# Slot attention in one block: context rows as values, fp32r updates, a second exponential

## The reference

```python
x_in = _ln(x, lnkv_g, lnkv_b)                  # x is the context here, 6404 rows
k = x_in @ wk + bk
v = x_in @ wv + bv
slots = q_mu + jnp.exp(q_logsig) * noise       # noise is the normed token
for _ in range(3):
    prev = slots
    q = _ln(slots, lnq_g, lnq_b) @ wq + bq
    logits = jnp.einsum('bnd,bkd->bnk', k, q) / scale
    attn = jax.nn.softmax(logits, axis=-1) + 1e-8      # over the slots
    attn = attn / jnp.sum(attn, axis=1, keepdims=True) # over the context
    upd = jnp.einsum('bnk,bnd->bkd', attn, v)
    slots = upd @ wu + bu + prev
    h = _ln(slots, lnm_g, lnm_b) @ w1 + b1
    slots = jax.nn.gelu(h, approximate=False) @ w2 + b2 + slots
    slots = _ln(slots + x_cls[:, None, :], lnp_g, lnp_b)
x = x + slots
```

## Time and profile before

| | |
|---|---|
| median of 3 runs | 3694.49 us (3694.09 to 3701.91) |
| profiled execution | 3696.8 us, its span 3695.0 us |
| TensorE busy | 3261.3 us (88%) |
| VectorE busy | 2541.0 us (69%) |
| ScalarE busy | 1522.6 us (41%) |
| GpSimd busy | 1656.7 us (45%) |

### The profile page before, as it was taken

How to read it: one execution, slowest core, us unless ns; L and a number is a source line. 1 busy time by engine, 2 the same in 40 slices (tenths; PEclk the granted TensorE clock), 3 DMA queues, 4 the chain that set the end, 5 groups by cost and what they waited for, 6 DMA issues and landing times. The chain is left out here.

```text
span 3695.0 us, 52448 instructions
## 1 busy us (share of the span) xinstructions
PE 3261.3 (88%) x18307; PEld 1830.0 (50%) x18307; DVE 2541.0 (69%) x4276; ACT 1522.6 (41%) x1875; POOL 1656.7 (45%) x1085
## 2 busy tenths in 40 slices
PE   3795969848734899999999999999999999999977
PEld 2463635523332455555555555555555555555435
DVE  6786868765324877687687777777777768768531
ACT  4231323324411344444444544444444444444432
POOL 1222212211122265565565566566556556556750
PEclk9896979956667999999999999999999999999988
DMA  1000000000031000000000000000000000000000
GB/s 59 0 0 1 0 0 0 0 12 1 1 106 49 3 1 1 1 4 1 1 4 1 1 4 1 1 1 4 1 1 4 1 1 2 1 1 1 1 25 6
DMA packets 20393, 27.92 MB, mean 8 GB/s; under 512 B 5064, under 2 KB 12368, under 8 KB 20048
## 3 DMA queue, kind: packets, MB, share of 16 engines
q1 hardware_dynamic: 18832, 21.83, 1.8%
q0 software_dynamic: 1344, 3.15, 0.3%
HBM read 21.30 MB, written 3.67 MB: 7 GB/s over the span
## 5 line engine op out<-in xcount | busy, mean ns | idle before, releaser
L2017 ACT ACTIVATE pair_probs<-banks 128x1024 f32<-128x1024 f32 (+1 forms) x944 | 965.5, 1026 | 1035.9 <-PE banks L1927 984.0
L2066 DVE TENSOR_REDUCE pair_peaks<-banks 128x1 f32<-128x512 f32 (+1 forms) x1800 | 1086.0, 666 | 271.7 <-PE banks L1909 258.2
L2159 POOL TENSOR_TENSOR pair_total_pool<-pair_total_pool,pair_probs 128x1536 f32<-128x1536 f32 x208 | 724.6, 3484 | 754.0 <-DVE pair_total L2080 748.8
L1950 PE MATMUL banks<-pair_probs,pair_values 128*64 128x512 f32 (+1 forms) x3776 | 873.1, 600 | 0.0
L1909 PE MATMUL banks<-pair_k_high,pair_q_high 64*128 64x512 f32 (+1 forms) x1920 | 567.0, 441 | 27.4 <-DVE pair_peaks L2059 14.9
L2148 POOL TENSOR_TENSOR pair_total_pool<-pair_total_pool,pair_probs 128x1024 f32<-128x1024 f32 x224 | 536.0, 2393 | 39.1 <-POOL pair_total_pool L2159 20.6
L2080 DVE TENSOR_TENSOR pair_total<-pair_total,pair_probs 128x512 f32<-128x512 f32 (+2 forms) x464 | 457.9, 987 | 94.6 <-ACT pair_probs L2017 69.4
L1950 PEld LDWEIGHTS banks<-pair_probs,pair_values 128*64 128x64 f32 (+1 forms) x3776 | 248.3, 136 | 473.0 <-issue 385.1
L1927 PE MATMUL banks<-pair_q_shift,pair_one_rows 64*128 64x512 f32 (+1 forms) x1888 | 475.7, 396 | 3.1 <-ACT pair_probs L2017 3.1
L1909 PEld LDWEIGHTS banks<-pair_k_high,pair_q_high 64*128 64x128 f32 x1920 | 262.6, 184 | 356.3 <-issue 211.7
L1927 PE MATMUL banks<-pair_q_high,pair_k_high 64*128 64x512 f32 (+1 forms) x1888 | 427.0, 391 | 0.0
(11 more groups left out here) (312 smaller groups left out, 3484.8 us busy)
## 6 DMA issues: line engine op xcount, KB each, us to landing
expert_w<-in_fc SPq DMA_DIRECT2D x32, 256.0 KB, 3.7
context_rows<-in_ctx SPq DMA_DIRECT2D x10, 320.0 KB, 5.7
dense_w<-in_We SPq DMA_DIRECT2D x2, 1024.0 KB
experts_in<-expert_zeros SPq DMA_DIRECT2D x1, 1024.0 KB, 3.9
expert_b<-in_fc_b SPq DMA_DIRECT2D x2, 512.0 KB, 4.9
expert_rows<-experts_in SPq DMA_DIRECT2D x16, 64.0 KB, 2.0
experts_out<-expert_result POOLq DMA_DIRECT2D x4, 256.0 KB, 4.3
row_parameters<-in_rows SPq DMA_DIRECT2D x1, 896.0 KB, 7.8
```

The lines of the kernel that those rows point to most:

```text
L1950: last = pe.matmul(out[heads[head], :], values[0:n, ring_of(h // 2, i // 4), i % 4, heads[head]], probs_of(h, i)[0:n, head, :], start=i == ...
L2017: act.activation(probs_of(h, i)[0:n], slot(e)[0:n], ACT.Exp, scale=1.0 / 8.0).then_inc(S["expd"].sem, 1)
L2066: v.reduce_max(peaks[:, head, t, b:b + 1], fill_bank(f, head)[:, 0:width(b)], axis=AX).then_inc(S["peaked"].sem, 1)
L2159: pool.tensor_tensor(pooled[:], pooled[:], three, ALU.add).then_inc(S["pooled"].sem, 1)
```

## The change

The whole slot stage becomes one block with a pipeline written out by hand; the three loops are unrolled.

Preparation: each piece of the context is normed by ScalarE alone, transposed from its rows and kept in `k.zT`. Gain and shift of the context's norm are folded into the key weights (`wk`, `bias`), so the keys come straight from `k.zT`. Values are not made. The update sums context rows instead, and a matrix `combined` (value weights times wu, with the gain folded in) is applied after. The last column of each normed row is set to 1: since a normed row sums to zero the matrix can do without that column, and it now carries the sum of the attention, so `total` and L655 go. The statistics of x, the first slots and the first queries are made between the pieces.

Loop: keys are read from `k_high` and `k_low` without the ring. ScalarE takes the exponential twice from the same bank, once in fp32 with its sum (L546) and once written as fp32r (L549). The difference of the two is the low part: VectorE makes 768 columns of it (L654), GpSimd 256 (L781). GpSimd weighs the row tile (L769), rounds it (L772) and takes its low part (L774), in the first iteration it also adds up the rows (L817), and at tile 4 it adds `bu` to the slots (L820). TensorE's update is three fp32r products for each half (L451 to L453), three tiles behind the scores.

Between loops: the work is cut into two halves of four token tiles, which ScalarE, TensorE, GpSimd and VectorE take in turn, with no block's end. The reciprocal comes from the projected column 128 (L725). In `causal_` and `pair_` code, semaphores of the ended stage are used again, and waits count from their totals.

```diff
@@ slot_scores_and_updates (before) @@
-                    for n, source in enumerate((k_high, k_low)):
-                        pool.tensor_copy(key[:, r, n, 0:parts], source[:, ds(i * P, parts)]).then_inc(staged_s.sem, 1)
...
-                    for c in range(2):
-                        last = pe.matmul(update[:, c, :], value[0:parts, r, :], probs[0:parts, r, c * 512:(c + 1) * 512],
-                                         start=first, stop=final)
...
-                    v.scalar_tensor_tensor(out=total[0:parts], in0=probs[0:parts, r, :], scalar=small[0:parts, r, 3:4],
-                                           in1=total[0:parts], op0=ALU.mult, op1=ALU.add).then_inc(total_s.sem, 1)
@@ slot_attention (after), TensorE @@
+                def add(it, i):
+                    g, n, r = it * N + i, rows_of_tile(i), i % RING
+                    wait(pe, "valued", g + 1)
+                    wait(pe, "copied", g + 1)
+                    wait(pe, "subbed", g + 1)
+                    wait(pe, "subbed_pool", g + 1)
+                    for c in range(2):
+                        bank = k.ps[:, 4 + c, :]
+                        pe.matmul(bank, value_high[0:n, r, :], probs_high[0:n, r, columns[c]], start=i == 0, stop=False)
+                        pe.matmul(bank, value_low[0:n, r, :], probs_high[0:n, r, columns[c]], start=False, stop=False)
+                        last = pe.matmul(bank, value_high[0:n, r, :], probs_low[0:n, r, columns[c]], start=False, stop=i == CT)
+                    done("added", last)
@@ ScalarE @@
+                def exponential(it, i):
+                    g, n, r = it * N + i, rows_of_tile(i), i % RING
+                    wait(act, "bias", g + 1)
+                    wait(act, "subbed", g - RING + 1)
+                    wait(act, "subbed_pool", g - RING + 1)
+                    done("expd", act.activation(probs[0:n, r, :], flat(scores[r][0:n]), ACT.Exp, bias=small[0:n, r, 1:2],
+                                                scale=SLOT_SCALE, accum_out=small[0:n, r, 2:3]))
+                    wait(act, "added", g - RING + 1)
+                    done("copied", act.activation(probs_high[0:n, r, :], flat(scores[r][0:n]), ACT.Exp, bias=small[0:n, r, 1:2],
+                                                  scale=SLOT_SCALE))
@@ VectorE @@
+                def subtract(it, i):
+                    g, n, r = it * N + i, rows_of_tile(i), i % RING
+                    wait(v, "copied", g + 1)
+                    wait(v, "added", g - RING + 1)
+                    done("subbed", v.tensor_tensor(probs_low[0:n, r, 0:SHARE], probs[0:n, r, 0:SHARE],
+                                                   probs_high[0:n, r, 0:SHARE].bitcast(F32), ALU.subtract))
@@ GpSimd @@
+                def weigh(it, i):
+                    g, n, r = it * N + i, rows_of_tile(i), i % RING
+                    wait(pool, "inverted", g + 1)
+                    wait(pool, "added", g - RING + 1)
+                    done("weighed", pool.tensor_tensor(value[0:n, r, :], rows[0:n, i, :], small[0:n, r, 3:4].to_broadcast([n, D]),
+                                                       ALU.mult))
+                    wait(pool, "weighed", g + 1)
+                    done("weighed_high", pool.tensor_copy(value_high[0:n, r, :], value[0:n, r, :]))
+                    wait(pool, "weighed_high", g + 1)
+                    done("valued", pool.tensor_tensor(value_low[0:n, r, :], value[0:n, r, :], value_high[0:n, r, :].bitcast(F32),
+                                                      ALU.subtract))
...
+                for it in range(ITERATIONS):
+                    for i in range(N):
+                        subtract(it, i)
+                        weigh(it, i)
+                        if it == 0:
+                            n = rows_of_tile(i)
+                            wait(pool, "counted", i)
+                            done("counted", pool.tensor_tensor(sums[0:n], sums[0:n], rows[0:n, i, :], ALU.add))
```

920 lines of the change are left out of this document (472 added, 448 removed).

## The result

The changed kernel takes 3572.38 us, median of 4 runs (3571.46 to 3576.22), against 3696.55 (3694.09 to 3701.91): ratio 0.9664, 95% interval 0.9647 to 0.9681. Its profiled span is 3571.0 us against 3695.0, so 124 us shorter where 92 were forecast. The time lies inside the range of 3545 to 3655.

A forecast was written before the change was run, and what follows sets the result against it. GpSimd, held back by VectorE on SBUF, was taken to bound the loops; 57 + 180 + 1 + 39 + 161 + 39 + 161 + 29 = 667 us for the stage against 758.8, so 3603 us, range 3545 to 3655.

The forecast's parts named there:

- the preparation: Before the first score: ScalarE longest at 3.75 us a piece, first score at 57 us instead of 117.6.
- The bound in the loops: Slot loops: GpSimd's chain of 2.05 us plus the block by VectorE's subtraction, period 2.95, above TensorE's 2.82.
- the 3.13: GpSimd's period in us a tile by another case's release time, end plus 115 ns; some 27 us above the forecast time.
- Rival 1: Slot loops: TensorE stays the bound, three loops of 150 us, 51 us less, 3552; chance 0.2.
- Iteration 1: First slot loop: the row sum adds 0.37 us to GpSimd's period, giving 3.32 and a loop of 179.9 against 162.
- TensorE's product: Slot loops: an fp32r product of 512 columns takes 0.235 us, twelve of them 2.82 us a tile.
- The bound of 65: Before the first score: first score at 65 us if TensorE runs at its lower clock and ScalarE waits for it.
- Gaps and end: Between and after loops: gaps 39 us against 59.75 and 57, the first 1 more; end 29 against 38.4.
- The rest: Causal layer, experts and perceiver behind the slot stage keep their code and their 2936 us.
- Rival 3: Slot loops: granted clock falls from 2.4 to 1.2 GHz, up to 5.64 us a tile, some 4015 us; chance 0.04.
- Rival 2: Slot loops: GpSimd needs 3.3 us a tile, 3.7 in the first iteration, 54 us more, 3657; chance 0.15.

The follow-up runs named there:

- The kernel with ten products: The changed kernel without the product of the keys' low part with the queries' high part in every score; 3565.01 us, one run.
- the fp32 update: The changed kernel with two plain fp32 update products a tile, without second exponential, low parts of probabilities or values, and subtractions; 3587.04 us, ratio 0.9704.
- the reordered kernel: The changed kernel with the same work before the first score in another order on each engine; 3561.69 us, ratio 0.9638.
- GpSimd has 512 columns: The changed kernel with the probabilities' subtraction split 512 columns each for VectorE and GpSimd instead of 768 and 256; 3604.00 us, ratio 0.9752.
- one-input scaling: The changed kernel with VectorE's 768-column subtraction replaced by a scaled copy of the probabilities, leaving out part of the computation; 3550.03 us, one run.

## Why the prediction was right in sign and 31 us too high in time

It forecast 3603 us, a gain of 92, and the gain was 124. That the time fell inside the range is in part owed to the range's width, and to the preparation, whose 11 us too few hid a quarter of the 43 us too many elsewhere.

- **The bound in the loops.** The exclusion of the two engines on SBUF was right. The step that failed is "GpSimd's period is 2.05 + 0.78 to 0.96 ... I take 2.95" and, with it, "GpSimd becomes the bound": that is so in iteration 1 only. The kernel with ten products shows 2.66, 0.29 less, in three parts. The upper end, "since three waits on other engines stand in its chain", cost 0.12: those waits were over when GpSimd came to them. The block is 0.71 and not 0.78 (L768 with 1.11, less 0.40). And the chain without it is 1.95 and not 2.05: a wait on GpSimd's own semaphore costs 0.07 to 0.08 us here (L768 to L771, L771 to L773), where I had taken 0.17 from the earlier trace rows, two times; the operations themselves and their overlaps give 0.09 of this back. Nor does the 3.13 hold that the prediction works out from the release time of another case.
- **Rival 1**, given 0.2, is what iterations 2 and 3 show: TensorE is the bound. Of its two reasons the first, shorter operations than expected, comes near, though it was the waits that were shorter. The second, "VectorE's subtraction falls into GpSimd's waits", is not what happened: L769 loses its full 0.72 in these loops. Its 150 for the first loop was 18 off, my 180 12.
- **Iteration 1.** Forecast 3.32, measured 3.11. By its starts (203.95 to 204.36) the row sum adds 0.41, not 0.37: 2.66 + 0.41 = 3.07; the last 0.04 are not accounted for, and with the phases of ten products it is 2.97. The step from 162 to a longer loop, the one loss of the change, was right: 168.0, against the 159.8 of the fp32 update.
- **TensorE's product** is 0.231, not 0.235: 2.77 instead of 2.82, 2.5 us a loop. A loop of 151.9 is 51 x 2.77 and 10.6 more, so rival 1's 150 stood close for iterations 2 and 3.
- **Preparation.** "The longest engine per piece is ScalarE ... 3.75" was true up to piece 6 (six steps from 10.56 to 32.48, 3.65 us each on average). It left out that VectorE's queue waits for side products of TensorE behind the same piece, and that its shift is held up by GpSimd's addition. The order of the queues is all of the 11 us: the reordered kernel comes to 56.1 against the 57 forecast. The bound of 65 was too low for it.
- **Gaps and end.** 37.1, 35.7 and 27.6 against 40, 39 and 29: the working stands. TensorE's eight projections took 2.59 and 2.05 us in gap 2 and at the end, where I had 3.75 from the earlier trace rows; in gap 1 they took 3.81, and its 2.9 us have another cause, which was not looked for.
- **The rest.** 5 us less in code that was not changed, 4 of them in the causal attention. The mean granted clock in the first 120 us behind the stage was 0.63 after and 0.59 before; nothing was done to show that this is the cause, and the same code took 2927.7 to 2935.8 us in the other changed kernels.
- **Rival 3**, the clock falling in the loops, came only as the 3.4 us at 0.50 in each loop, 1.6 us of time in loop 3. Outside of these stretches it was 1.00, also where TensorE was busy for 17.5 of 20 us with ten products (180 to 200). **Rival 2** would have needed a period of 3.3 in iterations 2 and 3; they have 2.77, and 2.83 even when GpSimd has 512 columns.

## What to carry to other kernels

Where two engines shut each other out in a periodic loop, count the block from the phases of their chains, with the waits that are already over left out, and see which engine's period is the longest within hundredths of a microsecond: here GpSimd's 2.66 under TensorE's 2.77 let a change of 0.35 us a tile through in two loops, worth 9 and 8 us of the 18, and its 3.11 turned it into a loss of 8 in the other. When passes merge into one block, write each queue down step by step and ask of every wait what the engine holds back that the other engine needs first; a few side products placed one or two pieces earlier, with one addition moved, were worth 11 us. Work that must be done once per tile by the fullest engine may be free elsewhere: an accumulator on an eviction gave 18 us.

## What the hardware showed that was not expected

- GpSimd's operation that is held back ends behind VectorE's reported end by its own time less 0.14 us: the cast 0.15 (0.29 alone), the weighing L769 0.25 to 0.26 (0.40), L774 0.31 to 0.33 (0.46), with a subtraction of 768 columns, one of 512, and a one-input scaling. So the block is VectorE's time from the moment at which GpSimd arrives, less 0.14: 1.05 of 1.23 in the earlier trace rows, 0.72 of 0.96 in the loops.
- The same holds the other way round: VectorE's operation loses what GpSimd's still has to run, less 0.12 to 0.15. L654 loses 0.12 of the 0.26 us until L781 ends in iteration 2, L653 0.36 of 0.50 with ten products, and the small L605 2.15 of 2.27 beside a GpSimd addition of 1024 columns. Both happen in one period: L781 delays L654 by 0.12 us, and L654 then delays L769 by 0.72.
- The scaling with one SBUF input holds GpSimd back as the subtraction with two does (0.71 instead of 0.40). VectorE's maximum over 1024 columns of PSUM does not: L781 takes 0.73 to 0.74 us beside it.
- An accumulator read is an operation of 0.19 us on ScalarE, behind an eviction as behind the exponential, but it moves the next one by 0.09 only: in the preparation the keys' high part starts 0.67 us behind the turned copy with the read between them, and 0.58 without.
